# Moving a tile's normalisation three slots earlier and the weight sums of a mixture layer from GpSimd to VectorE

## The chip, the cores and the metric

The kernel runs on one core of one Trainium2 chip. The metric is the device time of one execution in microseconds (us), median over the runs shown. Engines are named as in the profile: PE is TensorE (PEld its weight loads), DVE is VectorE, ACT is ScalarE, POOL is GpSimd, SP is the engine whose queue issues all the transfers.

## The reference, cut to what matters

```python
# x (16, 1024, 256); E = 8 experts, H = D = 256
x = x + gnn(layernorm(x), adj, W, a)
def ffn(x, ...):                                   # x is layernorm(x), reshaped per node
    w = softmax(mean(x, axis=0) @ Wr + br)         # one weight per node and expert
    h = relu(bn1(einsum('bfd,edh->bfeh', x, W1) + b1))
    h = relu(bn2(einsum('bfeh,ehk->bfek', h, W2) + b2))
    y = einsum('bfeh,ehd->bfed', h, Wo) + bo
    return einsum('bfed,fe->bfd', y, w)
x = x + ffn(layernorm(x), ...)
```

All is fp32. Each fp32 matrix product is made of three fp32r products: an operand is split into an upper part (`_hi`, a copy by ACT) and a lower part (`_lo`, operand minus upper, by DVE), and TensorE adds hi*hi, hi*lo and lo*hi.

## The kernel before, in words

The first part of the program is the attention layer (until about 715 us of the span). The change leaves it alone. The second part, `ffn_block`, works on 32 tiles of 512 rows. For each tile it runs 8 steps, one for each expert, so there are NS = 256 steps. Its order is written out by hand as slots `u` from -4 to 255. Each engine has a function `slot(u)`, which issues that engine's part of several steps at once:

- In slot u, PE computes the second layer of step u+2 (z2, two blocks of 6 matmuls of 512 columns), the last layer of step u (y, 21 matmuls of 256 columns), and the first layer of step u+4 (z1, again two blocks of 6).
- In slot u, ACT computes, in this order: the second relu of the first layer of step u+3, the two relus of the second layer of step u+2 (L1149), the upper part of h1 of step u+3 (L1185), the first relu of the first layer of step u+4, and the upper part of the seven operand sums of step u+2 (`second_upper`, L1163). What belongs to a tile or to a weight comes between or behind these.
- In slot u, DVE computes: the lower part of the operand sums of step u+1 (L1287), the product with the gate row of step u+2 (L1294, which needs the relus), the lower part of h1 of step u+3 (L1299, which the z2 of the next slot on PE waits for), and three operations for the sums of step u+2 (L1304, L1307, L1310).

"Slot k of a tile" below is the slot with u % 8 = k. The function `tile_due(u, at, ahead)` gives the tile u//8 + ahead if the slot is the tile's slot `at`.

The last layer is a Strassen form with 7 products instead of 8. It needs, for each expert's Wo, four sums of 128x128 blocks (S1 to S4, `weight_sums`, L962), then the upper part of seven blocks (`weight_upper`, L1170) and the lower part (L1264). These are made once in the first tile's slots and are kept in DRAM (`wo_scratch`). From step 8 on, they are loaded from there. In the kernel before, POOL makes the sums in slot u for expert u+3. ACT's `weight_upper(u+2)` is the last operation of ACT's slot, and DVE's lower part of expert u+1 is the first operation of DVE's slot. Two buffers hold the loaded Wo blocks: `wo_sums0` and the tile buffer `x1_sb[3]`.

A tile also needs its layer normalisation. DVE makes statistics of the tile after the next in slot 6 (L73, four at once) and the mean and variance at that slot's end (L80). POOL works out deviation and shift from them (L86 to L973). ACT makes the normalised rows of the next tile at the end of slot 0 (`normalise`, L1131, four operations of 128x256, waiting for `shift_ready`). PE transposes these rows in slot 1 and slot 2 (L994), after the slot's z2 and before its y. ACT and DVE split the transposed tile into `xT_hi` and `xT_lo` (L1124, L1227). Slots 0 and 1 hold DVE's combination of the previous tile's products, slots 4 and 5 the output addition (L1232) and the bias addition (L1239), and slot 7 the copies of the products out of PSUM (L1195 on ACT, L1319 on DVE).

SP's slot stores an expert's Wo operands once its lower part is ready (`wo_lo_ready`), then loads the next Wo, then the gate row of step u+4.

Of the kernel before, what the change touches and what calls it, by code (L numbers as in the profile page):

```python
# [23 lines left out]
ALU = mybir.AluOpType  # L24
# [3 lines left out]
P = 128  # L28
# [16 lines left out]
def bits(ap):  # L45

    return ap.bitcast(FP32)
# [9 lines left out]
class TileNorm:  # L57
# [10 lines left out]

    def statistics(self, dve, x1, x1_in, turn):

        dve.wait_ge(x1_in, DMA * turn)
        for s in range(self.CT):
            dve.bn_stats(self.stats[:, s, :], x1[:, s, :]).then_inc(self.stat, 1)  # L73
# [723 lines left out]
def ffn_block(nc, B, Wo, x1_dram, w_dram, wo_dram, out, ident, minus_half, node_table, w12_hi, w12_lo,  # L797
# [20 lines left out]
    with ctx:  # L818
# [14 lines left out]
        x1_sb = [x1_first] + [sb(f"ffn_x1{i}", [P, CT, D]) for i in range(1, XB)]  # L833
        wo_sums = [sb("wo_sums0", [P, 8, P]), x1_sb[3][:, :, :].rearrange("p s (h d) -> p (s h) d", d=P)]
        half_shift, shift = sb("ffn_half_shift", [P, CT]), sb("ffn_shift", [P, CT])
# [9 lines left out]
        prod = sb("products", [P, 7, HALF])  # L845
        comb = sb("combined", [P, 5, HALF])

        h2_rows = g2[:, 0:4, :].rearrange("p (k n) c -> p k (n c)", k=KB)
# [11 lines left out]
        stored = [sem(f"ffn_stored{i}") for i in range(XB)]  # L860
        sums_in = [sem(f"wo_sums_in{i}") for i in range(2)]
        ops_in, ops_stored = [sem(f"wo_ops_in{i}") for i in range(2)], [sem(f"wo_ops_stored{i}") for i in range(2)]
# [10 lines left out]
        def is_step(s):  # L873
            return 0 <= s < NS

        def tile_due(u, at, ahead):

            t = u // E + ahead
            return t if u % E == at and 0 <= t < TILES else None
# [4 lines left out]
        def _(sp):  # L884
            def load_sums(e):
                for m in range(KB):
                    sp.dma_start(wo_sums[e % 2][:, (1 - m):4:2, :],
                                 Wo[e].rearrange("(k p) d -> p k d", p=P)[:, :, m * P:(m + 1) * P]) \
                        .then_inc(sums_in[e % 2], DMA)

# [10 lines left out]
            def slot(u):  # L901
                e = u + 1
                if 0 <= e < E:

                    sp.wait_ge(S["wo_lo_ready"], e + 1)
                    sp.dma_start(wo_dram[e], bits(wo_ops[e % 2][:, :, :, :])).then_inc(ops_stored[e % 2], DMA)
                    if e + 2 < E:
                        load_sums(e + 2)
                s = u + 1
# [20 lines left out]
            for e in range(2):  # L930
                load_sums(e)
            load_x1(1)
            sp.wait_ge(S["wT_ready"], 1)
            sp.dma_start(w_dram.rearrange("e c n -> e (c n)"), wT_sb).then_inc(w_stored, DMA)
# [16 lines left out]
        def _(pool):  # L951
            def weight_sums(e):

                s, done = wo_sums[e % 2], 4 * e
                pool.wait_ge(sums_in[e % 2], DMA * KB * (e // 2 + 1))
                for dst, left, right, op in ((S1, A21, A22, ALU.add), (S3, A21, A11, ALU.subtract),
                                             (S2, S1, A11, ALU.subtract), (S4, A12, S2, ALU.subtract)):
                    if dst == S2:
                        pool.wait_ge(S["wo_sum_ready"], done + 1)
                    if dst == S4:  # L960
                        pool.wait_ge(S["wo_sum_ready"], done + 3)
                    pool.tensor_tensor(s[:, dst, :], s[:, left, :], s[:, right, :], op).then_inc(S["wo_sum_ready"], 1)  # L962

            def shift_rows(n):
# [11 lines left out]
            def slot(u):  # L976
                t = tile_due(u, 6, 2)
                if t is not None:
                    norm.deviation(pool, t + 1)
                    shift_rows(t + 1)  # L980
                if 2 <= u + 3 < E:
                    weight_sums(u + 3)

            for e in range(2):
                weight_sums(e)
            for u in range(-Z1, NS):
# [134 lines left out]
        def _(act):  # L1121
# [3 lines left out]

            def normalise(t):

                act.wait_ge(S["shift_ready"], t)
                wait(act, S["xT_psum"], 2 * t)
                for s in range(CT):  # L1130
                    last = act.activation(norm.xn[:, s, :], x1_sb[t % XB][:, s, :], ACT.Identity,  # L1131
                                          bias=shift[:, s:s + 1], scale=norm.rstd[:, s:s + 1])
                last.then_inc(norm.xn_ready, 1)

# [30 lines left out]
            def weight_upper(e):  # L1165

                act.wait_ge(S["wo_sum_ready"], 4 * (e + 1))
                wait(act, S["step_done"], e - 1)
                wait(act, ops_stored[e % 2], DMA * (e // 2))
                act.activation(wo_ops[e % 2][:, 0, :, :], wo_sums[e % 2][:, 1:8, :], ACT.Copy) \  # L1170
                    .then_inc(S["wo_hi_ready"], 1)

            def slot(u):
# [12 lines left out]
                if u == -2:  # L1186
                    copy_gate()
                if u == -1:
                    copy_gate_bias()
# [11 lines left out]
                second_upper(u + Z2)  # L1201
                t = tile_due(u, 0, 1)
                if t is not None and u >= 0:
                    normalise(t)
                if -2 <= u and u + 2 < E:
                    weight_upper(u + 2)
# [17 lines left out]
        def _(dve):  # L1224
# [19 lines left out]
            def combine(t, part):  # L1244
# [9 lines left out]
                else:  # L1254
                    dve.wait_ge(S["comb_ready"], COMBINES * t + 2)
                    put(comb[:, C22:C22 + 2, :], spread(comb[:, U3, :]), prod[:, P5:P5 + 2, :])
                    put(comb[:, C12, :], comb[:, U4, :], prod[:, P3, :])

            def slot(u):
                e = u + 1  # L1260
                if 0 <= e < E:

                    dve.wait_ge(S["wo_hi_ready"], e + 1)
                    dve.tensor_tensor(wo_ops[e % 2][:, 1, :, :], wo_sums[e % 2][:, 1:8, :],  # L1264
                                      bits(wo_ops[e % 2][:, 0, :, :]), ALU.subtract).then_inc(S["wo_lo_ready"], 1)
                for i in range(2):
# [11 lines left out]
                    if t is not None and u >= 0:  # L1278
                        residual(t, i)
                t = tile_due(u, 6, 2)  # L1280
                if t is not None:
                    norm.statistics(dve, x1_sb[t % XB], x1_in[t % XB], t // XB + 1)
                s = u + Z2 - 1
# [18 lines left out]
                if is_step(s):  # L1302
# [8 lines left out]
                        .then_inc(S["t4_ready"], 1)  # L1311
                t = tile_due(u, 6, 2)
                if t is not None:
                    norm.mean_var(dve, t + 1, False)
                t = tile_due(u, E - 1, 0)
                if t is not None and t < TILES - 1:
                    dve.wait_ge(S["step_done"], E * (t + 1))
                    wait(dve, S["out_psum"], 2 * t)
                    dve.tensor_copy(prod[:, P5:P3 + 1, :].rearrange("p q c -> p (q c)"),  # L1319
                                    m_ps[:, 2:4, :].rearrange("p k c -> p (k c)")[:, 0:3 * HALF]) \  # L1320
                        .then_inc(S["prod_ready"], 1)

            def softmax():
# [18 lines left out]
            for d, acc in enumerate((turn, z_ps[:, 2, :])):  # L1342
                lower_x(acc, 0, d)
            slot(-Z1)
            softmax()
# [55 lines left out]
```

## Time and profile before

| | us |
|---|---|
| median of 3 runs | 2927.73 (2926.43 to 2928.63) |
| profiled execution, own time | 2927.11 |
| its span | 2925.3 |
| PE busy in the span | 2812.7 |
| DVE busy | 2414.9 |
| ACT busy | 2141.2 |
| POOL busy | 703.6 |

The span is what the rows are measured in. It begins with the first instruction recorded and ends with the last one. Start times of rows count from its beginning. "Idle before" in a row is the time that the engine sat idle before that instruction, with what released it behind the arrow. Matmuls overlap, so a matmul's own duration is longer than its share of PE's time. The distance between the starts of two neighbours is what counts.

### The profile page before, as it was taken

The page shows a single profiled execution, that of the slowest core. Times are in us where ns is not written, and L with a number is a line of the kernel's source. Part 1 is how long each engine was busy: PE and PEld are TensorE (multiplying, and loading weights), DVE is VectorE, ACT ScalarE, POOL GpSimd, SP SyncE. Part 2 cuts the span into 40 slices and gives each one's busy share as a digit, 9 for nine tenths or more (in the row PEclk, how much of TensorE's full clock was granted, in tenths as well). Part 3 has the DMA queues.
Part 4 walks back from the last instruction along what each step waited for, and adds up shares of the span by engine and source line. Part 5 has one row for each costly group of instructions (what it writes and reads, how often), then busy time and mean ns, then how long its engine had stood idle before and what let it go on. Part 6 is the DMA issues. An engine that isn't in the chain of part 4 may idle for free.

```text
span 2925.3 us, 48929 instructions
## 1 busy us (share of the span) xinstructions
PE 2812.7 (96%) x17110; PEld 2478.9 (85%) x17110; DVE 2414.9 (83%) x3528; ACT 2141.2 (73%) x3035; POOL 703.6 (24%) x985
## 2 busy tenths in 40 slices
PE   7999999998889999999999999999999999999998
PEld 7989899998678888888888888888888888888887
DVE  7999999996678888888888888888888888888887
ACT  6889888887666676677776676677677777677665
POOL 5888888887100000000000000000000000000000
PEclk9999999999999999999999999999999999999999
DMA  4444444442445455545455445455455445445544
GB/s 145 155 158 152 151 158 151 148 154 93 124 147 156 151 165 159 150 164 160 146 159 160 150 156 160 147 165 160 153 160 160 148 157 161 152 153 161 150 156 136
DMA packets 159980, 445.25 MB, mean 152 GB/s; under 512 B 16016, under 2 KB 73784, under 8 KB 159808
## 3 DMA queue, kind: packets, MB, share of 16 engines
q1 hardware_dynamic: 159808, 442.96, 48.5%
q8 instruction: 108, 1.77, 0.2%
q14 instruction: 64, 0.52, 0.1%
HBM read 401.97 MB, written 40.93 MB: 151 GB/s over the span
## 4 chain that ended last, share of the span: by engine, by line
PE 70%; ACT 3%; DVE 2%; issue 1%; DMA 0%; ACTq 0%; DVEq 0%
PE z_ps L52 16%; PE z_ps L53 16%; PE z_ps L54 16%; PE m_ps L1019 7%; PE m_ps L1021 7%; PE m_ps L1022 7%; ACT ffn_xn L1131 2%; PE turn_ps L994 1%; PE turn_ps L1002 1%; DVE h_lo L1287 1%; DVE h_sums L1294 0%; DVE h_lo L1299 0%; ACT wo_ops L1170 0%; ACT h_hi L1163 0%; PE m_ps L1036 0%
## 5 line engine op out<-in xcount | busy, mean ns | idle before, releaser
L1149 ACT ACTIVATE h<-z_ps,bn_shift,bn_scale 128x512 f32<-128x512 f32 x1024 | 755.7, 775 | 615.0 <-PE z_ps L54 580.3
L1287 DVE TENSOR_TENSOR h_lo<-h_sums,h_hi 128x1792 fp32r<-128x1792 f32 x256 | 518.5, 2026 | 205.6 <-ACT h_hi L1163 202.4
L1019 PE MATMUL m_ps<-h_hi,wo_ops 128*128 128x256 f32 x1792 | 514.5, 287 | 4.0 <-DVE h_lo L1287 4.0
L1022 PE MATMUL m_ps<-h_hi,wo_ops 128*128 128x256 f32 x1792 | 503.9, 281 | 0.0
L1021 PE MATMUL m_ps<-h_lo,wo_ops 128*128 128x256 f32 x1792 | 503.6, 281 | 0.0
L1163 ACT ACTIVATE h_hi<-h_sums 128x1792 fp32r<-128x1792 f32 x256 | 435.4, 1701 | 43.7 <-DVE h_sums L1310 34.0
L86 POOL TENSOR_TENSOR ffn_vareps<-ffn_mv,ln_eps 128x4 f32<-128x4 f32 x32 | 6.4, 199 | 1888.5 <-DVE ffn_mv L80 1888.5
L1294 DVE TENSOR_TENSOR h_sums<-h,gate_row 128x1024 f32<-128x1024 f32 x256 | 313.8, 1226 | 146.9 <-ACT h L1149 127.0
L52 PE MATMUL z_ps<-h_hi,w_hi 128*128 128x512 f32 x1024 | 406.4, 397 | 12.0 <-DVE h_lo L1299 12.0
L52 PE MATMUL z_ps<-xT_hi,w_hi 128*128 128x512 f32 x1024 | 406.6, 397 | 2.3 <-ACT h L1149 1.4
L53 PE MATMUL z_ps<-xT_lo,w_hi 128*128 128x512 f32 x1024 | 405.5, 396 | 0.0
L53 PE MATMUL z_ps<-h_lo,w_hi 128*128 128x512 f32 x1024 | 405.4, 396 | 0.0
L54 PE MATMUL z_ps<-xT_hi,w_lo 128*128 128x512 f32 x1024 | 405.4, 396 | 0.0
L54 PE MATMUL z_ps<-h_hi,w_lo 128*128 128x512 f32 x1024 | 404.8, 395 | 0.0
L1019 PEld LDWEIGHTS m_ps<-h_hi,wo_ops 128*128 128x128 f32 x1792 | 339.4, 189 | 9.9 <-DVE h_lo L1287 4.2
L1021 PEld LDWEIGHTS m_ps<-h_lo,wo_ops 128*128 128x128 f32 x1792 | 339.4, 189 | 5.5
L1022 PEld LDWEIGHTS m_ps<-h_hi,wo_ops 128*128 128x128 f32 x1792 | 338.7, 189 | 0.0
L1299 DVE TENSOR_TENSOR h_lo<-h,h_hi 128x1024 fp32r<-128x1024 f32 x256 | 312.1, 1219 | 1.0 <-ACT h_hi L1185 1.0
L52 PE MATMUL attn_ps<-wh_hi,pT_hi 128*128 128x256 f32 x1024 | 306.5, 299 | 0.0
L53 PE MATMUL attn_ps<-wh_lo,pT_hi 128*128 128x256 f32 x1024 | 289.7, 283 | 0.0
L54 PE MATMUL attn_ps<-wh_hi,pT_lo 128*128 128x256 f32 x1024 | 289.6, 283 | 0.0
L1185 ACT ACTIVATE h_hi<-h 128x1024 fp32r<-128x1024 f32 x256 | 270.3, 1056 | 0.0
(149 smaller groups left out, 5485.4 us busy)
## 6 DMA issues: line engine op xcount, KB each, us to landing
wo_ops<-wo_scratch SPq DMA_DIRECT2D x248, 896.0 KB, 6.4
adj_sb<-in_adj SPq DMA_DIRECT2D x128, 512.0 KB, 3.5
gate_row<-w_scratch SPq DMA_DIRECT2D x256, 256.0 KB, 4.6
x_sb<-in_x SPq DMA_DIRECT2D x64, 256.0 KB, 2.8
x_scratch<-x_sb SPq DMA_DIRECT2D x128, 128.0 KB, 1.8
ffn_x<-x_scratch SPq DMA_DIRECT2D x32, 512.0 KB, 7.8
out<-ffn_x SPq DMA_DIRECT2D x31, 512.0 KB, 8.0
wo_scratch<-wo_ops SPq DMA_DIRECT2D x8, 896.0 KB, 4.2
```

The costliest lines, as they stand in the source:

```text
L52: pe.matmul(out, w_hi, x_hi, start=first, stop=False)
L53: pe.matmul(out, w_hi, x_lo, start=False, stop=False)
L54: return pe.matmul(out, w_lo, x_hi, start=False, stop=last)
L1019: pe.matmul(m_at(q), w_hi, x_hi[:, x, :], start=e == 0 and q in OPENERS, stop=False, skip_group_check=True)
L1021: pe.matmul(m_at(q), w_hi, x_lo[:, x, :], start=False, stop=False, skip_group_check=True)
L1022: done = pe.matmul(m_at(q), w_lo, x_hi[:, x, :], start=False, stop=e == E - 1, skip_group_check=True)
L1149: return act.activation(dst, src, ACT.Relu, bias=bn_shift[layer][:, col], scale=bn_scale[layer][:, col])
L1163: act.activation(h2_hi[s % 2][:, :, :], g2[:, 1:8, :], ACT.Copy).then_inc(S["h2_hi_ready"], 1)
L1185: act.activation(h1_hi[s % 2][:, :, :], h1[:, :, :], ACT.Copy).then_inc(S["h1_hi_ready"], 1)
L1287: dve.tensor_tensor(h2_lo[s % 2][:, :, :], g2[:, 1:8, :], bits(h2_hi[s % 2][:, :, :]), ALU.subtract) \
L1294: dve.tensor_tensor(h2_rows, h2[:, :, :], gate[s % 2][:, :].unsqueeze(1).to_broadcast([P, KB, BANK]), ALU.mult).then_inc(S["gated_ready"], 1)
L1299: dve.tensor_tensor(h1_lo[s % 2][:, :, :], h1[:, :, :], bits(h1_hi[s % 2][:, :, :]), ALU.subtract) \
```

## The change: what it does

1. `normalise` is split in two halves of two operations each. They are issued in slots 5 and 6 (for the tile after the next), in place of all four in slot 0 (for the next tile). In a slot it stands before `weight_upper`.
2. The statistics are made in slots 2 and 3, two rows each. Mean and variance, and POOL's work on them, come in slot 4. The statistics of tile 1 are made before slot -4.
3. `weight_sums` goes from POOL to DVE: experts 0 and 1 before slot -4, experts 2 and 3 in slot -2, experts 4 to 7 at the start of slots 2 to 5.
4. Four buffers hold Wo blocks (`sums_home`): two more lie in `prod` and `x1_sb[2]`. Experts 0 to 3 are loaded at once at the start, and expert e+3 is loaded once expert e is through.
5. The lower parts of experts 0 and 1 are made in slot -2, and that of expert u+1 at the end of DVE's slot u, for u from 1 to 6. The upper parts of experts 0 and 1 are made in slot -2 on ACT, after `copy_gate`.

```diff
@@ statistics(self, dve, x1, x1_in, turn, rows=None)
-        for s in range(self.CT):
+        for s in range(self.CT) if rows is None else rows:
@@ ffn_block
-        wo_sums = [sb("wo_sums0", [P, 8, P]), x1_sb[3][:, :, :].rearrange("p s (h d) -> p (s h) d", d=P)]
...
+        wo_sums = [sb("wo_sums0", [P, 8, P]), x1_sb[3][:, :, :].rearrange("p s (h d) -> p (s h) d", d=P),
+                   prod[:, 0:4, :].rearrange("p q (h d) -> p (q h) d", d=P),
+                   x1_sb[2][:, :, :].rearrange("p s (h d) -> p (s h) d", d=P)]
...
+        def sums_home(e):
+            return ((e - 1) % 3, (e - 1) // 3) if e else (3, 0)
@@ sync, slot(u)
-                    if e + 2 < E:
-                        load_sums(e + 2)
+                    if 1 <= e < E - 3:
+                        load_sums(e + 3)
...
             for e in range(2):
                 load_sums(e)
             load_x1(1)
+            for e in range(2, 4):
+                load_sums(e)
@@ gpsimd, slot(u)
-                t = tile_due(u, 6, 2)
+                t = tile_due(u, 4, 2)
                 if t is not None:
                     norm.deviation(pool, t + 1)
                     shift_rows(t + 1)
-                if 2 <= u + 3 < E:
-                    weight_sums(u + 3)
-
-            for e in range(2):
-                weight_sums(e)
@@ scalar
-            def normalise(t):
+            def normalise(t, half):
                 act.wait_ge(S["shift_ready"], t)
                 wait(act, S["xT_psum"], 2 * t)
-                for s in range(CT):
+                for s in range(half * CT // 2, (half + 1) * CT // 2):
                     last = act.activation(norm.xn[:, s, :], x1_sb[t % XB][:, s, :], ACT.Identity,
                                           bias=shift[:, s:s + 1], scale=norm.rstd[:, s:s + 1])
-                last.then_inc(norm.xn_ready, 1)
+                if half == 1:
+                    last.then_inc(norm.xn_ready, 1)
@@ scalar, slot(u)
                 if u == -2:
                     copy_gate()
+                    for e in range(2):
+                        weight_upper(e)
...
                 second_upper(u + Z2)
-                t = tile_due(u, 0, 1)
-                if t is not None and u >= 0:
-                    normalise(t)
-                if -2 <= u and u + 2 < E:
+                for i in range(2):
+                    t = tile_due(u, 5 + i, 2)
+                    if t is not None:
+                        normalise(t, i)
+                if 2 <= u + 2 < E and u >= 0:
                     weight_upper(u + 2)
@@ vector
+            def weight_sums(e):
...
+            def weight_lower(e):
+                dve.wait_ge(S["wo_hi_ready"], e + 1)
+                dve.tensor_tensor(wo_ops[e % 2][:, 1, :, :], wo_sums[sums_home(e)[0]][:, 1:8, :],
+                                  bits(wo_ops[e % 2][:, 0, :, :]), ALU.subtract).then_inc(S["wo_lo_ready"], 1)
+
             def slot(u):
-                e = u + 1
-                if 0 <= e < E:
-
-                    dve.wait_ge(S["wo_hi_ready"], e + 1)
-                    dve.tensor_tensor(wo_ops[e % 2][:, 1, :, :], wo_sums[e % 2][:, 1:8, :],
-                                      bits(wo_ops[e % 2][:, 0, :, :]), ALU.subtract).then_inc(S["wo_lo_ready"], 1)
+                if u == -2:
+                    for e in range(2):
+                        weight_sums(e + 2)
+                        weight_lower(e)
+                if 4 <= u + 2 < E:
+                    weight_sums(u + 2)
...
-                t = tile_due(u, 6, 2)
-                if t is not None:
-                    norm.statistics(dve, x1_sb[t % XB], x1_in[t % XB], t // XB + 1)
+                for i in range(2):
+                    t = tile_due(u, 2 + i, 2)
+                    if t is not None:
+                        norm.statistics(dve, x1_sb[t % XB], x1_in[t % XB], t // XB + 1, range(2 * i, 2 * i + 2))
...
-                t = tile_due(u, 6, 2)
+                t = tile_due(u, 4, 2)
                 if t is not None:
                     norm.mean_var(dve, t + 1, False)
...
+                if 2 <= u + 1 < E:
+                    weight_lower(u + 1)
@@ vector, before the slots
+            norm.statistics(dve, x1_sb[1], x1_in[1], 1)
+            for e in range(2):
+                weight_sums(e)
             slot(-Z1)
             softmax()
```

## Rows read from the trace of the kernel before

**Rows 1.** The page, its first section: busy time and share of each engine.
```profile
PE 2812.7 (96%) x17110; PEld 2478.9 (85%) x17110; DVE 2414.9 (83%) x3528; ACT 2141.2 (73%) x3035; POOL 703.6 (24%) x985
```

**Rows 2.** Waits, 860 to 2900 us: who waited for what, total, times, longest.
```profile
PE turn_ps L994 <- ACT ffn_xn L1131: 26.6, 29, 1.3
```

**Rows 3.** Timeline of PE, a tile's slot 1: start, duration, instruction, idle before.
```profile
1523.74 0.40 PE L54 MATMUL z_ps<-h_hi,w_lo 128*128 128x512 f32 x1
...
1525.03 0.66 PE L994 MATMUL turn_ps<-ident,ffn_xn 128*128 128x128 f32 x4 [0.90 <-ACT ffn_xn L1131]
```

**Rows 4.** Timeline of PE: z1 of slots 6 and 7, z2 of the slot after.
```profile
1569.66 0.40 PE L52 MATMUL z_ps<-xT_hi,w_hi 128*128 128x512 f32 x1
...
1577.72 0.40 PE L52 MATMUL z_ps<-xT_hi,w_hi 128*128 128x512 f32 x1
...
1580.53 0.39 PE L52 MATMUL z_ps<-h_hi,w_hi 128*128 128x512 f32 x1
```

**Rows 5.** Timeline of ACT: slots 0 and 1, slots 5 and 6.
```profile
1522.92 2.06 ACT L1131 ACTIVATE ffn_xn<-ffn_x,ffn_shift,ffn_rstd 128x256 f32<-128x256 f32 x4
1524.88 2.09 ACT L1149 ACTIVATE h<-z_ps,bn_shift,bn_scale 128x512 f32<-128x512 f32 x3
...
1564.49 1.70 ACT L1163 ACTIVATE h_hi<-h_sums 128x1792 fp32r<-128x1792 f32 x1 [0.50 <-DVE h_sums L1310]
1566.10 2.10 ACT L1149 ACTIVATE h<-z_ps,bn_shift,bn_scale 128x512 f32<-128x512 f32 x3
...
1572.30 1.70 ACT L1163 ACTIVATE h_hi<-h_sums 128x1792 fp32r<-128x1792 f32 x1 [0.25 <-DVE h_sums L1310]
```

**Rows 6.** Timeline of DVE: slot 1's gate product, then all of slot 6.
```profile
1527.07 1.23 DVE L1294 TENSOR_TENSOR h_sums<-h,gate_row 128x1024 f32<-128x1024 f32 x1 [1.99 <-ACT h L1149]
...
1566.23 2.02 DVE L1287 TENSOR_TENSOR h_lo<-h_sums,h_hi 128x1792 fp32r<-128x1792 f32 x1 [0.46 <-ACT h_hi L1163]
1568.38 1.23 DVE L1294 TENSOR_TENSOR h_sums<-h,gate_row 128x1024 f32<-128x1024 f32 x1
1569.53 1.22 DVE L1299 TENSOR_TENSOR h_lo<-h,h_hi 128x1024 fp32r<-128x1024 f32 x1
1570.66 0.68 DVE L1304 TENSOR_TENSOR h_sums<-h_sums 128x512 f32<-128x512 f32 x1
...
1571.84 0.42 DVE L1310 TENSOR_TENSOR h_sums<-h_sums 128x256 f32<-128x256 f32 x1
1572.18 0.37 DVE L80 BATCH_NORM_AGGREGATE ffn_mv<-ffn_stats 128x2 f32<-128x6 f32 x4
```

**Rows 7.** Timeline of PE, first tile: z2 of slots 0 and 8, slot 9's transposes.
```profile
754.79 0.40 PE L52 MATMUL z_ps<-h_hi,w_hi 128*128 128x512 f32 x1
...
837.28 0.40 PE L52 MATMUL z_ps<-h_hi,w_hi 128*128 128x512 f32 x1
...
850.42 0.44 PE L994 MATMUL turn_ps<-ident,ffn_xn 128*128 128x128 f32 x2 [2.12 <-ACT ffn_xn L1131]
```

**Rows 8.** Timelines of ACT and of DVE in slot 0 of the first tile.
```profile
756.84 0.93 ACT L1170 ACTIVATE wo_ops<-ffn_x 128x896 fp32r<-128x896 f32 x1
...
757.80 1.09 DVE L1264 TENSOR_TENSOR wo_ops<-ffn_x,wo_ops 128x896 fp32r<-128x896 f32 x1 [0.87 <-ACT wo_ops L1170]
```

**Rows 9.** One POOL line of the shift: count, shortest/median/longest ns, first and last start.
```profile
L970 POOL TENSOR_TENSOR ffn_half_shift<-ffn_half_shift,ffn_rstd x31: 199/1887/1891, 747.4 to 2787.7; 128x4 f32<-128x4 f32 x31
```

**Rows 10.** Start of the second part: tile 1's load and landing time, DVE's timeline.
```profile
717.16 0.47 SPq L896 DMA_DIRECT2D ffn_x<-x_scratch  x1
...
ffn_x<-x_scratch SPq DMA_DIRECT2D x1, 512.0 KB, 4.3
...
726.45 0.22 DVE L1326 TENSOR_TENSOR gate_expd<-turn_ps,br_sb 128x64 f32<-128x64 f32 x1 [7.92 <-PE turn_ps L1110]
...
730.41 1.40 DVE L73 BATCH_NORM_STATS2 ffn_stats<-ffn_x 128x6 f32<-128x256 f32 x4
...
741.52 1.23 DVE L1294 TENSOR_TENSOR h_sums<-h,gate_row 128x1024 f32<-128x1024 f32 x1 [9.71 <-DMA gate_row<-w_scratch]
```

More of the change, by code:

```diff
@@ L67, in __init__, with statistics @@
         self.rstd_ready, self.xn_ready = sem("ffn_rstd_ready"), sem("ffn_xn_ready")
-    def statistics(self, dve, x1, x1_in, turn):
+    def statistics(self, dve, x1, x1_in, turn, rows=None):
         dve.wait_ge(x1_in, DMA * turn)
-        for s in range(self.CT):
+        for s in range(self.CT) if rows is None else rows:
             dve.bn_stats(self.stats[:, s, :], x1[:, s, :]).then_inc(self.stat, 1)
@@ L860, in ffn_block @@
         stored = [sem(f"ffn_stored{i}") for i in range(XB)]
-        sums_in = [sem(f"wo_sums_in{i}") for i in range(2)]
+        sums_in = [sem(f"wo_sums_in{i}") for i in range(4)]
         ops_in, ops_stored = [sem(f"wo_ops_in{i}") for i in range(2)], [sem(f"wo_ops_stored{i}") for i in range(2)]
@@ L885, in load_sums @@
             def load_sums(e):
+                i, _ = sums_home(e)
                 for m in range(KB):
-                    sp.dma_start(wo_sums[e % 2][:, (1 - m):4:2, :],
+                    sp.dma_start(wo_sums[i][:, (1 - m):4:2, :],
                                  Wo[e].rearrange("(k p) d -> p k d", p=P)[:, :, m * P:(m + 1) * P]) \
-                        .then_inc(sums_in[e % 2], DMA)
+                        .then_inc(sums_in[i], DMA)
             def load_gate(s):
@@ L951, in _ @@
         def _(pool):
[L952 to L962, printed above, removed]
             def shift_rows(n):
@@ L1169, in weight_upper @@
                 wait(act, ops_stored[e % 2], DMA * (e // 2))
-                act.activation(wo_ops[e % 2][:, 0, :, :], wo_sums[e % 2][:, 1:8, :], ACT.Copy) \
+                act.activation(wo_ops[e % 2][:, 0, :, :], wo_sums[sums_home(e)[0]][:, 1:8, :], ACT.Copy) \
                     .then_inc(S["wo_hi_ready"], 1)
@@ L1257, in combine @@
                     put(comb[:, C12, :], comb[:, U4, :], prod[:, P3, :])
-            def slot(u):
-                e = u + 1
-                if 0 <= e < E:
-                    dve.wait_ge(S["wo_hi_ready"], e + 1)
-                    dve.tensor_tensor(wo_ops[e % 2][:, 1, :, :], wo_sums[e % 2][:, 1:8, :],
-                                      bits(wo_ops[e % 2][:, 0, :, :]), ALU.subtract).then_inc(S["wo_lo_ready"], 1)
+            def weight_sums(e):
+                i, turn_of = sums_home(e)
+                s, done = wo_sums[i], 4 * e
+                dve.wait_ge(sums_in[i], DMA * KB * (turn_of + 1))
+                for dst, left, right, op in ((S1, A21, A22, ALU.add), (S3, A21, A11, ALU.subtract),
+                                             (S2, S1, A11, ALU.subtract), (S4, A12, S2, ALU.subtract)):
+                    if dst == S2:
+                        dve.wait_ge(S["wo_sum_ready"], done + 1)
+                    if dst == S4:
+                        dve.wait_ge(S["wo_sum_ready"], done + 3)
+                    dve.tensor_tensor(s[:, dst, :], s[:, left, :], s[:, right, :], op).then_inc(S["wo_sum_ready"], 1)
+            def weight_lower(e):
+                dve.wait_ge(S["wo_hi_ready"], e + 1)
+                dve.tensor_tensor(wo_ops[e % 2][:, 1, :, :], wo_sums[sums_home(e)[0]][:, 1:8, :],
+                                  bits(wo_ops[e % 2][:, 0, :, :]), ALU.subtract).then_inc(S["wo_lo_ready"], 1)
+            def slot(u):
+                if u == -2:
[4 more added lines that the diff above has]
+                    weight_sums(u + 2)
                 for i in range(2):
```

## The prediction

> **What bounds the kernel now.** The page comes first: PE is busy for 96% of the span, DVE for 83%, ACT for 73% [rows 1]. So PE's gaps are what can be won, and a share of the whole span does not say where they are. The list of waits from 860 us on names one reason only: the transposes of slot 1 wait for ACT's normalised rows, 29 times in 29 tiles [rows 2]. The timeline of PE gives the size of one. The last z2 matmul of that slot starts at 1523.74. A matmul of z takes 0.23 of PE (12 of z2, 12 of z1 and 21 of y fill the 8.06 us below), so the transposes were due at 1523.97. They start at 1525.03 [rows 3]: 1.06 us lost in each tile. A slot without extras takes 8.06 (1569.66 to 1577.72) [rows 4]. Four transposes are 0.66 long, of which the last is 0.33, so they cost 4 x 0.11 = 0.44 [rows 3].
>
> The first tile is different. PE's z2 starts at 754.79 in slot 0 and at 837.28 in slot 8 [rows 7], 82.5 us, where PE alone needs 8 x 8.06 + 0.9 (eight transposes) = 65.3. So 17.2 are lost, and another 2.28 at the first transposes after it (due 837.28 + 8.06 + 12 x 0.233 = 848.14, came at 850.42) [rows 7]. The reason is a loop, which the timelines of ACT and DVE show. From DVE's last sum L1310 to ACT's L1163 it is 0.46, L1163 holds ACT for 1.61 [rows 5, 6]. Then `weight_upper` runs, and DVE's lower part of the weight starts 0.96 after it [rows 8]. That part holds DVE for 1.01 (1.09 less the 0.08 by which followers overlap, as 1.23 becomes 1.15 at L1294). Only then come h_lo 2.15, and 1.15, 1.13 and 1.18 to the next L1310 [rows 6]. Together 9.65, over PE's 8.06, and normalisation, `xT_lo`, bias or statistics come on top in slots 0 to 6.
>
> **The change in the later tiles.** The wait of slot 1 goes, since the rows are ready two slots before. Gain 1.06 x 29 = 30.7.
>
> What is late next is ACT's queue in slots 5 and 6. Half a normalisation takes (1524.88 - 1522.92)/2 = 0.98 [rows 5]. It stands between L1163 and the three relus. Two things wait for the last relu: DVE's gate product L1294, by 0.10 (1524.88 + 2.09 to 1527.07) [rows 5, 6], and PE's z1, whose bank it frees, for which I take the same 0.10.
> - Slot 5's half starts at 1566.10. The relus end at 1569.18 and the gate product starts at 1569.28 in place of 1568.38, 0.90 late [rows 5, 6]. z1 is due at 1569.66 [rows 4]: no stall, 0.4 to spare.
> - DVE carries the delay on: L1310 and ACT's L1163 of slot 6 are 0.90 late, L1163 at 1573.20 [rows 5, 6]. It ends at 1574.81, the second half at 1575.79, the relus at 1577.89. z1 may start at 1577.99, due 1577.72 [rows 4]: a new stall of 0.27 in slot 7.
> - Behind it the gate product starts at 1577.99 and h1's lower part at 1579.14. z2 may follow that by 1.3 (1.22 long, and 0.1), at 1580.4, due 1580.53 + 0.27. The copies out of PSUM and DVE's combination in slots 7 and 0 use up the rest: z2 of slot 1 comes within 0.1 of its due time. From slot 1 on the old normalisation is missing and the queues catch up.
>
> Bounds of the new stall: 0, if PE follows the relu more closely and the sums round the other way, and 0.66, if slot 6's spare 0.39 isn't there. I take 0.27, every term of which but the 0.10 is a row. Cost 29 x 0.27 = 7.8, net gain 22.9.
>
> The statistics are 1.40 for four [rows 10], now 0.70 in each of slots 2 and 3. They go ahead of h_lo, where DVE idles for L1163 anyway: from L1310 to h_lo it is 0.46 + 1.74 [rows 5, 6], of which L1310 itself takes 0.34, so 1.85 are idle. `xT_lo` (0.6, as the other 512 column rows less the overlap) and half the statistics fit. Uncovered they would cost 0.7 in a slot. POOL's shift chain has one operation of 1.9 [rows 9] and four shorter ones, and now starts a whole slot before its reader. SP issues nothing new in these tiles. All at nothing.
>
> **The change in the first tile.** `weight_lower` moves to the slot's end, where its upper part is a slot old. It runs in the 1.85 of idle time: free, 1.01 otherwise. `weight_sums` comes to DVE. No row shows a 128x128 operation there. The 512 and 256 column rows of 0.68 and 0.42 [rows 6] give 0.29 for 128 by their slope, and with two of the four waiting for the one before, 1.1 for a call. Bounds: 0.9, and 1.7 if 128 columns cost what 256 do.
>
> The Trainium skill ("VectorE: DVE Perf Modes", the section on the TRN2 errata) speaks against many small operations: it gives (N+151)/0.96 ns for an fp32 tensor_tensor, so over half of a 128 column one would be fixed. Its estimate is 0.29 us for one and 1.16 for four. For N = 1792 it gives 2.02, and the trace agrees with 2.02. With its price the sum would move by less than 0.3.
>
> I walk the slots with these terms. On ACT: L1163 1.61, half a normalisation 0.98, `weight_upper` 0.85 (0.93 less the overlap), three relus 2.10. On DVE: 2.15, 1.15, 1.13, 1.18, 0.34; in front 1.1 (sums, slots 2 to 5), 0.6 (`xT_lo` or bias, slots 2 to 5), 0.70 (statistics, slots 2, 3); at the end 1.01 (lower part, from slot 1) and 0.37 (mean, slot 4) [rows 6].
> - Slots 0 to 2: PE keeps its pace. z2 starts at 762.9 in slot 1, 771.4 in slot 2, 779.9 in slot 3.
> - DVE has 5.95 + 1.01 + 1.1 + 0.6 + 0.70 = 9.4 to do in slots 2 and 3, over PE's 8.5 and 8.06, and its lead of some 2 us runs out. h1's lower part of slot 3 starts at 787.2, z2 of slot 4 at 788.5: 0.5 lost.
> - Slots 4 and 5: the last relu stands behind L1163 and `weight_upper`, and z1 is late by 0.9 and 0.6.
> - Slot 6: `weight_upper(7)` and half a normalisation stand ahead of the relus. z1 at 813.3, due 811.4: 1.9.
> - Slot 7: the second half, 0.65.
>
> The stalls are 4.6 together. z2 of slot 8 starts near 824.9 in place of 837.28: gain 12.4. With the 2.28 of the late transposes, 14.7.
>
> **The start.** DVE now waits for tile 1's load before slot -4. It is issued at 717.16 and takes 4.3 [rows 10]. Then statistics 1.4, two calls of sums 2.2 and the mean 0.4: DVE is free at 725.5. The softmax L1326 starts at 726.45, after 7.92 idle [rows 10]. Covered by 0.9. If the two further Wo loads hold the tile back by 2 (as many bytes as the tile itself, in half its time), 1 us is uncovered. In slot -2 DVE idles for 9.71 until the gate row lands at 741.52 [rows 10]. Two sums (2.2) and two lower parts (2.0), the last behind ACT's two upper parts, end about 1 before that. ACT's half normalisation of slot -3 holds up `copy_gate`, and with it the gate row, by 0.1. SP stores an expert later, at DVE's slot end, and the gate row's load behind it still has over a slot until its use. Cost 0.1.
>
> **Sum.** 22.9 + 14.7 - 0.1 = 37.5. The profiled execution took 2927.11, which gives 2889.6. The median of the runs is 0.6 above it, so 2890, 1.3% faster.
>
> **The rivals.**
> - *No new stall.* PE keeps its pace from slot 0 on: 17.2 + 2.3 + 30.7 = 50.2, so 2878. For it: the 0.27 is a difference of long sums. Against it: DVE's 9.4 in the first tile's slots. Chance 0.12.
> - *The wait moves from slot 1 to slot 7.* The stall there is 0.8 to 1.06, because slot 6's 0.4 to spare is missing or the copies in slot 7 come late too. The later tiles give 0 to 7.5 and the first 14.7: 2906 to 2913. For it: both halves enter a loop of ACT and DVE that gets no time back before slot 0. Against it: the walk. Chance 0.15.
> - *Slower.* The halves come through to PE in full, 1.96 a tile, since the loop of ACT and DVE, and not PE, sets the pace from slot 5 on. That is 29 x (1.96 - 1.06) = 26 lost less 14.7: 2939. It decides from a new stall of 1.06 + 14.7/29 = 1.57 a tile. Against it: a plain loop is 0.46 + 1.74 + 2.15 + 1.15 + 1.13 + 1.18 = 7.81, under PE's 8.06 [rows 5, 6]. Chance 0.04.
> - *No change to be measured.* The wait moves in full, the sums cost 1.7 a call and the start 2, so that both parts cancel. Chance 0.03.
> - My forecast has the rest, 0.66, from 2883 to 2901 (stall 0 to 0.66; sums 0.9 to 1.7).
>
> The range that leaves out 2 in 10 is 2879 to 2907. A measurement of this kernel can tell 0.2%, 5.9 us, from no change. Faster by more: 0.12 + 0.66 + 0.15 = 0.93; within: 0.03; slower: 0.04.
>
> **What would show it.** In the later tiles the transposes L994 have left the list of waits, a tile is 0.8 shorter, and one new gap of 0.2 to 0.5 stands before z1 in slot 7, with ACT's relus L1149 as its releaser. In the first tile z2 of slot 8 starts near 825, and PE's largest gap is before z1 of slot 6. DVE's sums are rows of 0.29. The softmax starts at 726.5 and the first gate product near 741.6. The prediction is wrong if the gap of slot 7 is over 0.7, if z2 of slot 8 comes after 829, or if the softmax is late.

## The result, and the profile after

The changed kernel takes 2882.37 us (median; 2880.69 to 2883.41), the kernel before in the same session 2927.68 (2926.43 to 2928.63). The ratio is 0.9846, with a 95% interval of 0.983 to 0.9862: 45.3 us or 1.5% faster. The prediction was 2890 with a range of 2879 to 2907. It forecast 37.5 us of gain, so 7.8 were missing. The profiled execution took 2883.41, 1.04 over the median. Its span is 2881.6, against 2925.3 before.

The page of the changed kernel, its first section:

```profile
span 2881.6 us, 48960 instructions
...
PE 2809.0 (97%) x17110; PEld 2482.4 (86%) x17110; DVE 2415.4 (84%) x3560; ACT 2133.3 (74%) x3035; POOL 685.5 (24%) x953
```

PE and DVE are as busy as before [rows 1]. DVE has 32 instructions more (eight calls of four sums) and POOL 32 fewer. Of the 43.7 us between the two spans, 40.0 are idle time of PE; its busy time is 3.7 less.

**Later tiles.** The list of PE's waits from 860 to 2850 us is empty after: the transposes have left it [rows 2], and nothing has come in their place. The distance from one tile's first z2 to the next one's falls from 67.41 to 66.29 (medians), 1.12 a tile and 32.5 over 29 tiles. Taken slot by slot, slot 1 falls from 9.62 to 8.53 and the others stay within a few hundredths. Slots 5 to 7 of the changed kernel, timelines of ACT and of PE:

```profile
1541.56 1.70 ACT L1157 ACTIVATE h_hi<-h_sums 128x1792 fp32r<-128x1792 f32 x1
1543.17 1.08 ACT L1124 ACTIVATE ffn_xn<-ffn_x,ffn_shift,ffn_rstd 128x256 f32<-128x256 f32 x2
1544.15 2.09 ACT L1143 ACTIVATE h<-z_ps,bn_shift,bn_scale 128x512 f32<-128x512 f32 x3
...
1550.24 1.70 ACT L1157 ACTIVATE h_hi<-h_sums 128x1792 fp32r<-128x1792 f32 x1 [0.68 <-DVE h_sums L1327]
1551.85 1.07 ACT L1124 ACTIVATE ffn_xn<-ffn_x,ffn_shift,ffn_rstd 128x256 f32<-128x256 f32 x2
1552.84 2.09 ACT L1143 ACTIVATE h<-z_ps,bn_shift,bn_scale 128x512 f32<-128x512 f32 x3
```

```profile
1547.08 0.40 PE L52 MATMUL z_ps<-xT_hi,w_hi 128*128 128x512 f32 x1
...
1555.14 0.40 PE L52 MATMUL z_ps<-xT_hi,w_hi 128*128 128x512 f32 x1
```

The halves (L1124) stand where the prediction put them. The relus behind the second half end at 1552.84 + 2.09 = 1554.93, and z1 of slot 7 starts at 1555.14, exactly 8.06 after the one before. That is 0.21 after the relus. Less the 0.10 that the prediction allows from relu to z1, 0.1 is to spare, where the prediction had 0.27 too little.

**First tile.** PE's z2 of slots 0 and 8, and z1 of slot 6, the largest gap; then ACT ahead of that z1:

```profile
759.43 0.39 PE L52 MATMUL z_ps<-h_hi,w_hi 128*128 128x512 f32 x1
...
816.92 0.50 PE L52 MATMUL z_ps<-xT_hi,w_hi 128*128 128x512 f32 x1 [1.40 <-ACT h L1143]
...
828.51 0.40 PE L52 MATMUL z_ps<-h_hi,w_hi 128*128 128x512 f32 x1
```

```profile
811.35 1.70 ACT L1157 ACTIVATE h_hi<-h_sums 128x1792 fp32r<-128x1792 f32 x1 [0.68 <-DVE h_sums L1327]
812.95 1.08 ACT L1124 ACTIVATE ffn_xn<-ffn_x,ffn_shift,ffn_rstd 128x256 f32<-128x256 f32 x2
813.94 0.94 ACT L1164 ACTIVATE wo_ops<-wo_sums 128x896 fp32r<-128x896 f32 x1
814.78 2.09 ACT L1143 ACTIVATE h<-z_ps,bn_shift,bn_scale 128x512 f32<-128x512 f32 x3
```

Eight slots take 69.1 where they took 82.5 [rows 7], and the late transposes of slot 9 [rows 7] are gone: 13.4 + 2.3. In slots 4 to 7 the first z1 starts 0.9, 0.5, 1.7 and 0.6 after the matmul before it. Without a stall that distance is 0.12, so 0.8, 0.4, 1.6 and 0.5 are lost. The last relu of slot 6 stands behind half a normalisation and `weight_upper`, as walked.

**Start.** z2 of slot 0 is 4.64 later than in the profile of before (759.43 against 754.79). Of this, 0.57 lies ahead of the second part (its preceding stage ends at 710.27, before at 709.70). Most of the rest, 3.4, is slot -1: from its z2 to that of slot 0 it is 14.21, against 10.86. In that stretch PE ran at a lower granted clock. The table by stretch, first of the changed kernel (start and end, length, PE, PEld, DVE, ACT and POOL with counts, granted clock, DMA share, GB/s), then of the kernel before:

```profile
752.00:759.00 7.00, 7.00 (x18) 5.04 (x17) 4.59 (x7) 3.66 (x5) 0.00 (x0) 0.51 0.72 256
```

```profile
752.00:759.00 7.00, 7.00 (x37) 5.93 (x38) 6.06 (x9) 6.38 (x7) 2.94 (x4) 1.00 0.35 102
```

18 matmuls in 7 us against 37, at 0.51 (the lower level, 1.2 GHz) against 1.00.

The sum of the two profiles: 32.5 + 13.4 + 2.3 - 4.6 = 43.6, and the spans differ by 43.7.

### The profile page after: what moved, and what is told of

It reads as the page before. It is cut to its first block, busy times and chain, and to the rows that moved or that the text cites. A ratio compares the mean times of both kernels' runs of the same rounds, so it can differ in the third digit from the quotient of the medians.

```text
span 2881.6 us, 48960 instructions
## 1 busy us (share of the span) xinstructions
PE 2809.0 (97%) x17110; PEld 2482.4 (86%) x17110; DVE 2415.4 (84%) x3560; ACT 2133.3 (74%) x3035; POOL 685.5 (24%) x953
## 4 chain that ended last, share of the span: by engine, by line
PE 73%; ACT 1%; DVE 1%; issue 0%; DMA 0%; ACTq 0%; DVEq 0%
PE z_ps L52 17%; PE z_ps L53 16%; PE z_ps L54 16%; PE m_ps L1012 7%; PE m_ps L1014 7%; PE m_ps L1015 7%; PE turn_ps L987 1%; PE turn_ps L995 1%; ACT h L1143 0%; PE m_ps L1029 0%; DVE h_lo L1304 0%; DVE h_sums L1311 0%; DMA gate_row<-w_scratch 0%; DVE h_lo L1316 0%; PE turn_ps L1103 0%
```

## The experiments

Each time is a median, with the ratio to the kernel before in its own session (2927.2 to 2928.8 throughout) and the ratio's 95% interval.

**1. The normalisation part alone, on the kernel before.**

```diff
-                t = tile_due(u, 0, 1)
-                if t is not None and u >= 0:
-                    normalise(t)
+                for i in range(2):
+                    t = tile_due(u, 5 + i, 2)
+                    if t is not None:
+                        normalise(t, i)
```
(with the statistics, mean and shift at slots 2 to 4 as in the change; the weights stay as before)

> The kernel before with the normalisation part alone (halves in slots 5 and 6, statistics in 2 and 3, mean in 4); the weights as before. Theory 1 (the two parts are separate, and the later tiles gain the whole wait because ACT's delay in slots 5 to 7 just fits): the tiles' interval falls from 67.4 to 66.3, 29 x 1.13 = 32.7, and the first tile gives about 2, so 2893. Theory 2 (my prediction's: a new stall of 0.27 stands in slot 7): interval 66.6, 23 and 2, so 2903. Theory 3 (the gain comes from the weights' move, which takes POOL off DVE's memory access and DVE off the queue): under 10, 2918 or more.

2893.72, ratio 0.9883 [0.9866, 0.9899]: 34.1 faster. A tile is 66.29, as with the whole change.

**2. The weight part alone.** The changed kernel with the normalisation back in slot 0 and its statistics in slot 6.

```diff
-                for i in range(2):
-                    t = tile_due(u, 5 + i, 2)
-                    if t is not None:
-                        normalise(t, i)
+                t = tile_due(u, 0, 1)
+                if t is not None and u >= 0:
+                    for i in range(2):
+                        normalise(t, i)
```

> The changed kernel with the normalisation put back to slot 0 and the statistics to slot 6. Theory 1: interval of the tiles 67.4 as in the kernel before, z2 of the first tile's slots 0 to 8 about 68 to 69 apart (82.5 before), so 2915. Theory 3: interval near 66.3, and 2890 or less.

2915.98, ratio 0.9958 [0.9941, 0.9975]: 11.8 faster. A tile is 67.41 again, and the wait is back in the list of PE's waits, 860 to 2850 us:

```profile
PE turn_ps L987 <- ACT ffn_xn L1124: 26.1, 29, 1.0
```

34.05 + 11.79 = 45.8, against 45.3 for both at once: the two parts add up.

**3 and 4. All four normalising operations in one slot, 6 or 7.**

```diff
-                    t = tile_due(u, 5 + i, 2)
+                    t = tile_due(u, 6, 2)
```
(and with 7)

> The changed kernel with all four operations of the normalisation in slot 6. Theory 1 by the row of the usual tile: ACT's upper sums start 2.53 after z1 of slot 6, then 1.61 + 1.96 + 2.10 + 0.10 = 8.30, over 8.06: a stall of 0.25 before z1 of slot 7 in each tile, 29 x 0.25 = 7, so 2889 to 2890. Rival (the same work in a neighbouring slot costs the same, there is room to spare): 2882.

> The changed kernel with all four operations in slot 7, behind the copy of the products. Theory 1: the upper sums start 3.19 after z1 there, so 3.19 + 1.61 + 1.96 + 2.10 + 0.10 = 8.96, a stall of 0.9 before z1 of slot 0 in each tile, 26 in all, so 2908. Rival (only the transposes' own wait for the rows cost time, and here the rows are ready a slot ahead): 2882, no gap.

In slot 6: 2890.44, 0.9873 [0.9856, 0.9889]. A tile is 66.57, 0.28 more than with halves, all of it in slot 7. In slot 7: 2911.01, 0.9942 [0.9926, 0.9959]. A tile is 67.27, and the list of PE's waits has a new member, of which the timeline shows one:

```profile
PE z_ps L52 <- ACT h L1143: 19.6, 29, 0.7
```

```profile
1506.91 0.50 PE L52 MATMUL z_ps<-xT_hi,w_hi 128*128 128x512 f32 x1 [0.68 <-ACT h L1143]
```

So a stall before z1 exists, and it appears when 2 us of ACT come late enough. With half in slot 5 and half in slot 6 there is none.

**5. Each half doubled,** into a buffer that nothing reads.

```diff
+                for s in range(half * CT // 2, (half + 1) * CT // 2):
+                    act.activation(spare[:, s % 2, :], x1_sb[t % XB][:, s, :], ACT.Identity,
+                                   bias=shift[:, s:s + 1], scale=norm.rstd[:, s:s + 1])
```

> The changed kernel with each half of the normalisation doubled: two more operations of the same kind go to a spare buffer that nothing reads. Theory 1 (ACT's queue between the upper sums and the relus reaches PE with all that goes beyond z1's due time): slot 6 has 2.53 + 1.61 + 1.96 + 2.10 + 0.10 = 8.30, a stall of 0.25, slot 7 one of about 1.6, 1.9 a tile, 54 in all and some 4 in the first tile, so 2941. Rival (ACT idles 2 us in each slot, which takes the extra work up): under 10, so 2892 or less.

2938.54, 1.0037 [1.0022, 1.0052]: slower than before. A tile is 68.19, with one slot at 9.67 and one at 8.35:

```profile
PE z_ps L52 <- ACT h L1147: 39.9, 30, 1.7
```

ACT has 1.96 more in these two slots, and the tile is 1.90 longer: the second 2 us come through to PE nearly in full, as in the rival that ends slower, where the first 2 cost nothing in the later tiles. The spare time of the loop is used up by the change itself.

**6. The lower part of the weight at the front of DVE's slot,** where it waits for ACT's upper part of the same slot.

```diff
+                if 2 <= u + 1 < E:
+                    weight_lower(u + 1)
                 for i in range(2):
...
-                if 2 <= u + 1 < E:
-                    weight_lower(u + 1)
```

> The changed kernel with the lower part of expert u+1 put back to the front of DVE's slot u, behind the sums, so that it waits for the upper part that ACT has just made. Theory 1 (what the first tile gains is that wait): slots 1 to 6 take 9.6 to 10.9 each in place of 8.1 to 9.7, 8 to 10 in all, so 2891. Rival (the end of one slot and the front of the next are neighbours in DVE's queue, so the place costs nothing, and the first tile's gain is from the normalisation and the preloaded buffers): under 1, 2883.

2891.80, 0.9876 [0.9859, 0.9892]. That is 9.4 more than the changed kernel, and slots 0 to 8 take 78.75 against 69.08: without the new place of this one instruction most of the weight part's 11.8 is lost. No run moves it alone on the kernel before, so it isn't shown that the place is enough without the preloaded buffers. Its wait in the timeline of DVE:

```profile
791.38 1.09 DVE L1272 TENSOR_TENSOR wo_ops<-wo_sums,wo_ops 128x896 fp32r<-128x896 f32 x1 [2.41 <-ACT wo_ops L1164]
```

**7 and 9. The sums back on POOL, from four buffers,** behind the shift's operations (7) or ahead of them (9). The edit of 7, with DVE's calls taken out and POOL's calls for experts 0 to 3 (before the slots and in slot -3) left out here:

```diff
                 t = tile_due(u, 4, 2)
                 if t is not None:
                     norm.deviation(pool, t + 1)
                     shift_rows(t + 1)
+                if 4 <= u + 2 < E:
+                    weight_sums(u + 2)
```

> The changed kernel with the weight sums back on GpSimd, still from four preloaded buffers. Theory 1 (DVE's load of 9.4 in the first tile's slots 2 to 5 makes the stalls of slots 4 to 6): DVE is 0.93 a slot lighter, the gaps before z1 of slots 4 and 5 (0.8 and 0.4) shrink or go, and z2 of slots 0 to 8 are 67.5 to 68.2 apart in place of 69.1; the time is 2881, not to be told from 2882. Rival (sums on GpSimd slow DVE's operations, as its 256 column rows of 0.57 in place of 0.42 beside them may show): z2 of slots 0 to 8 are 69 or more apart.

2886.55, 0.9858 [0.9842, 0.9875], where 2881 was expected. One gap explains it, 5.1 from the matmul before to z1 of slot 5 in place of 0.5: the sums of expert 6 stand behind POOL's wait for the mean of slot 4, and ACT's copy behind them. POOL and ACT:

```profile
802.30 0.96 POOL L86 TENSOR_TENSOR ffn_vareps<-ffn_mv,ln_eps 128x4 f32<-128x4 f32 x1 [17.14 <-DVE ffn_mv L80]
...
806.37 1.81 POOL L972 TENSOR_TENSOR products<-products 128x128 f32<-128x128 f32 x4
```

```profile
808.21 0.95 ACT L1184 ACTIVATE wo_ops<-products 128x896 fp32r<-128x896 f32 x1 [4.54 <-POOL products L972]
```

> The last kernel (weight sums on GpSimd) mended: in GpSimd's slot the sums of expert u+2 now stand ahead of the shift's chain and not behind its wait for slot 4's mean. Theory 1: the gap of 5.1 before z1 of slot 5 goes, z2 of slots 0 to 8 are 67.5 to 68.5 apart (69.1 in the changed kernel), 2881. Rival (contention with DVE): 69 or more.

2882.83, 0.9844 [0.9829, 0.9859]: the same as the changed kernel. Slots 0 to 8 take 69.58, where 67.5 to 68.5 was expected and the rival (contention) had 69 or more. Before z1 of slots 4 to 7 the distances are 0.8, 0.5, 2.0 and 0.6, against 0.9, 0.5, 1.7 and 0.6 with the sums on DVE. Taking 1.0 a slot off DVE gained nothing. This doesn't clear DVE's load as a cause: over slots 2 to 5 DVE was busy for 31.5 us in place of 33.2, and not for 4 less, since both engines are slower side by side. But before its gate product DVE now sits idle, waiting for ACT's relu (0.60 in slot 4, 0.86 in slot 5), and the stall of slot 6 is there all the same. DVE and POOL of this kernel:

```profile
807.08 1.31 DVE L1315 TENSOR_TENSOR h_sums<-h,gate_row 128x1024 f32<-128x1024 f32 x1 [0.86 <-ACT h L1163]
808.31 1.48 DVE L1320 TENSOR_TENSOR h_lo<-h,h_hi 128x1024 fp32r<-128x1024 f32 x1
809.71 0.94 DVE L1325 TENSOR_TENSOR h_sums<-h_sums 128x512 f32<-128x512 f32 x1
```

```profile
806.85 4.13 POOL L972 TENSOR_TENSOR wo_sums<-wo_sums 128x128 f32<-128x128 f32 x4
```

Alone these take 1.22 and 0.68 [rows 6] and, the four sums, 1.81.

**8. The kernel before once more,** one execution.

> The kernel before, unchanged, for a second profile. Open: in the profile of the changed kernel z2 of slot -1 and of slot 0 are 14.2 apart, in the one of before 10.9, and PE's granted clock is 0.51 from 752 to 759 us in the one and 1.00 in the other. Theory A (the second low stretch comes with the time at which PE starts again, and not with the change): here too it may show, and slot -1 may take 14.2. Theory B (the change causes it): 10.9 again, and the clock 1.00 from 752 to 759.

2927.58. This time slot -1 took 14.28, as after, and its stretch was slow too:

```profile
752.00:759.00 7.00, 7.00 (x19) 5.06 (x18) 5.64 (x7) 3.90 (x4) 2.46 (x4) 0.55 0.41 125
```

So the slow stretch isn't the change's. The other profiles bear this out: in all ten without matmuls in the wait, other than the first one of the kernel before, slot -1 takes 14.2 to 14.6 and 752 to 759 is granted 0.51 to 0.57. z2 of slots 0 and 8 came at 758.9 and 838.7, 79.8 apart in place of 82.5. With the same slow stretch in both, the first tile's slots gain 10.7 and the start costs 0.5. What the stretch costs does depend on the kernel: the kernel before was 4.1 later at slot 0 than in its first profile, but only 1.4 later at slot 8 and 0.5 at the end, since its slots 0 to 2 took 30.6 in place of 33.6.

**10. PE kept busy through its longest wait,** with 24 matmuls in slot -1 into a bank that nothing reads.

```diff
+            def keep_busy(n):
+                for i in range(n):
+                    pe.matmul(m_ps[:, 2, :], w12_hi[:, 0, 0, 0:P], xT_hi[0][:, 0, :], start=i == 0, stop=i == n - 1)
...
+                if u == -1:
+                    keep_busy(24)
```

> The changed kernel with 24 matmuls of 512 columns in PE's slot -1, ahead of its wait for h1's lower part, into a PSUM bank that nothing reads before it is overwritten. They fill 5.6 of the 6.9 us in which PE waits for the gate row. Theory A (the granted clock is at half behind that idle time, and that makes slot -1 longer): the clock stays at 1.00, z2 of slots -1 and 0 are 9.5 to 11 apart in place of 14.2, so 2878 to 2879. Rival (the low stretch has nothing to do with PE's idling): 2882, or later if the 24 matmuls run at half speed and hold up z2.

2879.23 (2878.28 to 2880.49), 0.9836 [0.9822, 0.9849]. That is 3.1 under the changed kernel, less than the times alone can tell, but the trace shows it: slot -1 takes 11.10 in place of 14.21 (11.09 and 11.08 in experiments 11 and 12, which have the same matmuls). The stretches of the changed kernel and of this one:

```profile
738.00:745.00 7.00, 0.69 (x3) 0.21 (x2) 5.19 (x8) 1.10 (x2) 0.00 (x0) 0.77 0.27 80
```

```profile
738.00:745.00 7.00, 6.43 (x28) 4.88 (x27) 5.76 (x11) 0.78 (x1) 0.00 (x0) 1.00 0.34 120
752.00:759.00 7.00, 7.00 (x34) 5.80 (x33) 5.34 (x8) 5.67 (x7) 0.00 (x0) 0.87 0.82 281
```

The wait ahead of z2 (6.9 us from the start of the last matmul to that of z2, 6.5 of it idle, for h1's lower part, which waits for the gate row) stands in front of the slow stretch. With PE busy in the wait, 752 to 759 was granted 0.87, and 0.76 and 0.93 in experiments 11 and 12.

**11. Experiments 9 and 10 together, and the first tile's halves in slots 6 and 7, behind `weight_upper`.**

```diff
-                    t = tile_due(u, 5 + i, 2)
+                    t = tile_due(u, (6 if 0 <= u < E else 5) + i, 2)
```

> The changed kernel with the last two edits (sums on GpSimd ahead of the shift's chain, 24 matmuls in the wait) and a third: in the first tile the normalisation's halves stand in slots 6 and 7, behind the upper part of the weight. Theory: the third takes most of the 1.6 before z1 of slot 6, 3.5 to 4.5 come from the clock and 1 from the sums: 2875 to 2877, the fastest. Rival: each gain is used up by DVE's lead, and the sum is that of keep_busy alone, 2878 or more.

2880.12, 0.9837 [0.9824, 0.985], where 2875 to 2877 was expected. The distance to z1 of slot 6 fell from 1.7 to 1.04, but in slot 8 it rose from 0.12 to 0.76, and slots 0 to 8 still took 68.69. The rival (2878 or more) was right. The extra work of ACT was only moved to another slot of the same loop.

**12. The extras of ACT moved to where it idles.** With experiment 10's matmuls, from slot 0 on, the half normalisation and `weight_upper` go from behind the upper sums to behind `h1_hi`, ahead of the first relu. There ACT waits for DVE or PE, for 2.1 us in most slots of the later tiles and for about 1 in the first.

```diff
+                if u >= 0:
+                    tile_work(u)
                 first_relu(u + Z1, 0)
...
-                for i in range(2):
-                    t = tile_due(u, 5 + i, 2)
-                    if t is not None:
-                        normalise(t, i)
-                if 2 <= u + 2 < E and u >= 0:
-                    weight_upper(u + 2)
+                if u < 0:
+                    tile_work(u)
```
(`tile_work` holds the removed lines)

> keep_busy with one more edit: from slot 0 on, the halves of the normalisation and the upper part of the weight stand on ACT behind the upper part of h1 and ahead of the first relu of z1, where ACT idles about 2 us in each slot, and no longer between the upper sums and the relus. Theory 1a (the gaps of 0.8, 0.4, 1.6 and 0.5 before z1 of slots 4 to 7 come from the loop on ACT and DVE, 0.46 + 1.61 + 0.84 + 2.10 + 0.10 + 3.45 = 8.56 with the weight's upper part, 9.5 with half a normalisation too): they go, z2 of slots 0 to 8 are 65.4 to 66.3 apart in place of 69.1, and the time is 2876. The later tiles stay at 66.29. Theory 1b, as my prediction had it (DVE's load in slots 2 to 5 makes them): the gaps of slots 4 and 5 stay, 68 or more, 2878.

2875.91 (2874.5 to 2877.09), 0.9822 [0.9808, 0.9835]: 52.9 under the kernel before, and some 6.5 under the changed kernel. Against experiment 10 it is 3.3, of which slots 0 to 8 are 2.9: they take 66.2 in place of 69.1, where the prediction counted 65.3 for PE alone. All z1 of these slots start 0.12 after the matmul before. A later tile stays at 66.29. In its timeline of ACT the weight's copy stands behind `h1_hi`, and the relus follow the upper sums directly. The list of PE's waits from 750 to 830 has one member left:

```profile
789.66 2.10 ACT L1150 ACTIVATE h<-z_ps,bn_shift,bn_scale 128x512 f32<-128x512 f32 x3
791.64 1.07 ACT L1195 ACTIVATE h_hi<-h 128x1024 fp32r<-128x1024 f32 x1
793.37 0.95 ACT L1171 ACTIVATE wo_ops<-products 128x896 fp32r<-128x896 f32 x1 [0.67 <-DMA wo_scratch<-wo_ops]
```

```profile
PE z_ps L52 <- DVE h_lo L1330: 0.4, 1, 0.4
```

## Why the prediction was right, and where it was off

**The wait of slot 1 (forecast 1.06 a tile): right.** It measures 1.09, and experiments 1 and 2 tie it to the place of the normalisation.

**The new stall of slot 7 (forecast 0.27 a tile, 7.8): this step failed.** The usual tile has none. The mechanism holds: ACT's queue delays the relus, and z1 waits for them once they are late enough (experiments 3 to 5). What was wrong is the row that the walk started from. The upper sums of slot 5 at 1564.49 [rows 5] belong to an unusual tile, in which the gate product had started 0.35 later than in the others: in slot 5 it is the only one of 30 tiles. The tile before it, in the kernel before: the gate product of slot 5 (DVE, then that of the quoted tile), the z1 (PE) and the upper sums (ACT) that follow it:

```profile
1492.81 1.23 DVE L1294 TENSOR_TENSOR h_sums<-h,gate_row 128x1024 f32<-128x1024 f32 x1 [0.64 <-ACT h L1149]
...
1560.58 1.23 DVE L1294 TENSOR_TENSOR h_sums<-h,gate_row 128x1024 f32<-128x1024 f32 x1 [0.99 <-ACT h L1149]
```

```profile
1494.20 0.39 PE L52 MATMUL z_ps<-xT_hi,w_hi 128*128 128x512 f32 x1
```

```profile
1496.73 1.71 ACT L1163 ACTIVATE h_hi<-h_sums 128x1792 fp32r<-128x1792 f32 x1
```

The upper sums start 2.53 after z1. In the quoted tile z1 is at 1569.66 - 8.06 = 1561.60 [rows 4], so they start 2.89 after it. With 2.53 the walk gives relus that end 0.36 earlier, and the 0.27 becomes 0.09 to spare: no stall. Over the tiles of the changed kernel the upper sums of slots 5 and 6 start 2.53 and 3.17 after z1 (medians), and the last relu starts 1.61 and 0.97 before the next z1. It ends 0.84 and 0.20 before it. Only three tiles are longer than 66.4 (66.57, 66.59 and 66.46). In the first two the gate product of slot 5 or of slot 6 started 0.35 late, and slot 7 takes 8.34 and 8.37 in place of 8.06. For such a tile the forecast was right. In experiment 12 the gate product is 0.35 late in the same two tiles, and neither is longer than 66.3. Why a few tiles start the gate product late is open.

**The statistics, the mean and the shift at nothing: right,** to the accuracy of a tile of 66.29, which holds no gap.

**The sums on DVE (forecast 1.1 a call, 0.9 to 1.7): right.**

```profile
776.65 1.01 DVE L1267 TENSOR_TENSOR wo_sums<-wo_sums 128x128 f32<-128x128 f32 x4
```

Four take 1.01, and one by itself has 0.27 to 0.29. The Trainium skill's formula, which the prediction took from "VectorE: DVE Perf Modes" (TRN2 errata), has 0.29 for one: the trace agrees.

**The first tile's slots (forecast 12.4): 13.4 between the two profiles, 10.7 when both have the slow stretch** (experiment 8). The forecast lies between the two, and that it is so near to the first is in part luck: the 82.5 that it started from is 79.8 in the other execution of the same kernel. z2 of slot 8 started at 828.5, 3.6 later than forecast and just short of the 829 named as a sign of being wrong, because slot 0 started 4.6 later. The late transposes gave the forecast 2.3. The place of the lower part carries most of it (experiment 6), as the loop of 9.65 said.

**The stall of z2 in slot 4 (forecast 0.5): it didn't come.** The prediction had 9.4 of DVE's work in slots 2 and 3, which uses up its lead. DVE's slot 3 took 9.14 (from the lower part at 784.78 to the next at 793.92), its lead was just used up, and nothing was lost: z2 starts 0.23 after the matmul before, and 1.30 after h1's lower part. DVE, then PE:

```profile
791.27 1.22 DVE L1316 TENSOR_TENSOR h_lo<-h,h_hi 128x1024 fp32r<-128x1024 f32 x1
```

```profile
792.57 0.47 PE L52 MATMUL z_ps<-h_hi,w_hi 128*128 128x512 f32 x1
```

**The stalls of z1 in slots 4 to 7 (forecast 0.9, 0.6, 1.9, 0.65): right in size** (0.8, 0.4, 1.6, 0.5), and in cause: the prediction put them down to the relus behind ACT's extra work. (The expectation of experiment 12 gives DVE's load as the prediction's cause, which it was for z2 of slot 4 alone.) The relus stand in a loop through ACT: 0.46 from the last sum to the upper sums, 1.61, `weight_upper` 0.84, relus 2.10, 0.10 to the gate product, and 3.45 back to the last sum: 8.56. With half a normalisation more it is 9.5. Taking the extras out of this loop, and leaving DVE's work as it was, removed all four (experiment 12). DVE's load is not far behind: in slot 5 it has no idle time, and from last sum to last sum it takes 8.75 in both kernels (here 802.13 to 810.88). The 0.4 before z2 of slot 6 in experiment 12, which waits for DVE, fits that.

**The start (forecast a loss of 0.1): 4.6 in the profile, 0.5 against experiment 8.** The softmax was covered, as forecast, but later:

```profile
727.56 0.23 DVE L1345 TENSOR_TENSOR gate_expd<-turn_ps,br_sb 128x64 f32<-128x64 f32 x1 [2.31 <-PE turn_ps L1103]
```

DVE was free at 725.2 and PE came last, 1.1 later than before [rows 10]. Of this 0.57 came from the stage before. In experiment 8 the unchanged kernel starts the softmax at 727.20, so no more than 0.4 is left for the change. The first gate product started at 742.80, forecast 741.6.

Between the profiles the later tiles gave 9.6 more than forecast (7.8 of it the stall, 1.8 that the wait was 1.12 and not 1.06), the first tile 1.0 more, and the start 4.5 less: 43.7 in place of 37.5. So the start hid half of the error of the later tiles, which is luck. The other 1.6 up to the medians' 45.3 is where the two profiled executions lie beside their medians. The rival "no new stall" was half right: none in the usual later tile, 3.3 us of them in the first tile.

## What to carry to other kernels

Before a walk rests on one tile's rows, compare their distances to PE with those of several tiles: here 0.35 in one row decided between a stall in every tile and none. When an engine's queue is part of a loop that sets the pace, extra work is free at the point where that engine itself waits; moved to another slot but to the same point of the loop, it takes the stall along. Two parts of a change that act in different stages can be costed and summed separately: 34.1 and 11.8 gave 45.3 together.

## What was not expected of the hardware

- Some 7 us after a wait with 6.5 us of idle time PE ran 7 us at a granted clock of 0.51 (1.2 GHz, the lower level), with 18 matmuls in place of 37. In ten of eleven profiles with this wait it was 0.51 to 0.57. 24 matmuls in the wait raised it to 0.87 and took 3.1 us off that slot. The one execution that escaped (1.00, the first of the kernel before) had a wait as long, 6.35 us idle; why it escaped is open.
- DVE and POOL slow each other: beside POOL's sums DVE's operation of 1.22 took 1.48 and that of 0.68 took 0.94, and POOL's four sums of 1.81 took up to 4.13. The Trainium skill ("GPSIMD Engine Reference", section 1) says that the two share their interfaces to SBUF and contend when DVE has two inputs there, as here; these rows agree.
